# Two transformer blocks on one core: the order of all five engines' work written anew

## The chip, the cores and the metric

The kernel runs on one core of a Trainium2 chip. A core has five engines with instruction streams of their own: TensorE (PE, matmuls; PEld is its weight load), VectorE (DVE), ScalarE (ACT), GpSimd (POOL) and SyncE (SP, which here only issues transfers). They wait for each other by semaphores. Each engine takes its instructions strictly in the order in which they stand in the program, so an instruction that waits holds up all that stand behind it. Transfers between the chip's memory and the core's buffers run on 16 DMA engines and are issued by SyncE and by ScalarE. The metric is the device time of one execution in microseconds (us), the median over several.

## The reference

x has 8 batches of 512 tokens with 256 features. Two layers are added to it, one after the other, and each is a conditioned map and a feed-forward net with ternary weights and 8-bit activations:

```python
x = x + L0_ffn(L0_cond(x, ids0))
x = x + L1_ffn(L1_cond(x, ids1))

L0_cond: h = relu(x @ W1[id] + b1[id]); y = x + h @ W2[id] + b2[id]     # 256 -> 64 -> 256
         layernorm(y) * gamma[id] + beta[id]
L0_ffn:  h = gelu(bitlinear(z, W1, b1)); bitlinear(h, W2, b2)           # 256 -> 1024 -> 256
L1_cond: x @ W[id].T + b[id]                                            # 256 -> 256
L1_ffn:  h = bitlinear(y, w1); h = conv3(h) along the tokens, one filter per channel, + bias
         h = silu(h); bitlinear(h, w2)                                  # 256 -> 1024 -> 256
bitlinear(x, W): W is rounded to -1, 0, 1 times its mean absolute value;
                 x to whole numbers of -128..127 by the largest absolute value of each token
```

The ids pick one of 10 (layer 0) or 8 (layer 1) sets of weights for each batch.

## The kernel before, in words

A batch b is four tiles of 128 tokens; two tiles are a pair p, and the arguments of the functions are (b, p) or (b, tile j). The functions are named after one step each, and each belongs to one engine.

Layer 0, for a batch: SyncE loads the adapter's weights (`load_adapter_weights` L337, `load_second` L345) and gamma and beta (`load_norm` L352), ScalarE issues the loads of x, once transposed (`load_rows` L502) and once as tokens (`load_tokens` L507). PE does `adapter_in` (L1177) and `adapter_out` (L1189), ScalarE the relu between them (`adapter_hidden`). VectorE adds (`add_adapted` L923), centres (`centre` L934) and normalises (`normalise` L943), with the variance from ScalarE (`squares`) and GpSimd (`negative_mean`, `inverse_deviation`). Then the pair is quantised: `absmax_z`, `scale_z`, `inverse_z` on VectorE, `round_z` on ScalarE, `transpose_z` on PE, `untranspose_z` on ScalarE. For each tile PE multiplies (`up1` L1216), ScalarE does `gelu` (L543) into one of two buffers g1, VectorE finds the largest value (`absmax1` L968) and the scale, GpSimd rounds (`round1` L754) into r1, SyncE issues a transposing transfer (`transpose1` L367), PE does `down1` (L1231) and VectorE adds the result to the tokens (`final1` L984). `gelu(b, j)` waits for `round1` of the tile two before, since g1 has two buffers.

Layer 1, for a batch: PE transposes the tokens (`transpose_x` L1262) and multiplies in float32 (`linear` L1279), ScalarE copies in and out (`lead` L574, `evacuate` L580), VectorE finds the scales (`absmax_y` L998), GpSimd rounds (`round_y` L780), PE transposes (`transpose_y`, `spread_scales`), ScalarE copies (`lead_q` L586, `lead_scales`). Then in eight blocks f of 128 channels: `up` on PE (L1326), `dequant` on VectorE (L1014), the three taps of the convolution as `last_tap` on ScalarE (L601), `first_tap` on VectorE (L1021) and `middle_tap` (L798) and, for two blocks at once, `tap_sum` (L808) on GpSimd. For each tile: `transpose_conv` on PE, `silu` on ScalarE, `absmax2` on VectorE, `round2` on ScalarE, `transpose2` by SyncE, `down2` on PE, `final2` on VectorE (L1046) and `store2` by SyncE.

The two layers overlap only at the seam, where the last batches of layer 0 and the first of layer 1 are worked on together. The four weight matrices (1024 KB each) are loaded at the start (`load_weights` L362: n = 0 by ScalarE, 1 to 3 by SyncE), summed by ScalarE (`weight_sum`), totalled by PE (`weight_total`), and made ternary (`weight_scale` and `ternary(0)` on VectorE; `scaled_weights`, `clipped_weights` and `ternary` on ScalarE and GpSimd for the others).

The order of the work is written out by hand for each engine. `run` (L314) goes through four parts:

```python
def run(opening, slot1, closing, slot2):
    opening()
    for s in range(5, B + 1):
        slot1(s)
    closing()
    for s in range(3, B + 4):
        slot2(s)
```

`opening` and `closing` are lists of calls, `slot1` and `slot2` are lists that are repeated for each s, with `on(op, s - 2, j)` calling op for batch s - 2 if there is such a batch. Nothing but these lists sets the order; the waits are inside the functions.

## Time and profile before

| | |
|---|---|
| median of 3 runs | 321.74 us (318.56 to 323.08) |
| the profiled execution | a span of 319.6 us from the first to the last instruction; no time of its own is given beside the span |
| busy: PE, VectorE, ScalarE, GpSimd | 264.5, 276.6, 240.6, 259.2 us |
| moved by transfers | 39.50 MB, 124 GB/s in the mean |

The profile is of one execution. A busy time is the sum of an engine's instructions' durations; an instruction that is held up by another engine once it has started counts as busy. "idle before" in a group of instructions is the time in which the engine had nothing running before them, with what ended most of it. The windows give busy times in stretches of the span, with the granted clock of PE (1.00 is 2.4 GHz) and the DMA engines' share. A transfer's "us to landing" runs from its issue to its arrival.

### The profile page before, as it was taken

To read this page: it belongs to the slowest core of one execution; us is meant where nothing else is said; L and a number is where in the kernel's file an instruction comes from. 1 tells how busy PE (TensorE), PEld (TensorE's weight loads), DVE (VectorE), ACT (ScalarE), POOL (GpSimd) and SP (SyncE) were. 2 spreads that over 40 slices of the span, in tenths; PEclk is the share of its full clock that TensorE was granted. 3 is DMA by queue.
4 is the path that set the end of the run, shared out by engine and by line. 5 is a ranking of instruction groups with operands and counts; after the bars stand their busy time and mean duration, and the time that the engine had idled before them with its cause. 6 is when DMAs were issued, how large, how long until landed. Compare 5 with 4: busy or idle time off the path is not lost. (4 is left out here: it accounts for less than half of the span.)

```text
span 319.6 us, 6460 instructions
## 1 busy us (share of the span) xinstructions
PE 264.5 (83%) x1676; PEld 179.7 (56%) x1700; DVE 276.6 (87%) x606; ACT 240.6 (75%) x366; POOL 259.2 (81%) x402
## 2 busy tenths in 40 slices
PE   6679878869798887999889797989899898967574
PEld 6234334535455454566656665868587686745452
DVE  0778988896899989955899999999999999999671
ACT  4588897966776487567566888889989888978770
POOL 2567899996898988759999999998989799898310
PEclk9977799999999999999999999999999999999997
DMA  7995773579496368454430333445436373444764
GB/s 249 320 363 118 222 197 76 113 159 213 100 215 126 75 87 178 69 100 91 44 66 2 60 74 66 118 98 91 111 93 122 70 98 82 101 98 100 120 145 115
DMA packets 90745, 39.50 MB, mean 124 GB/s; under 512 B 73005, under 2 KB 88141, under 8 KB 90710
## 3 DMA queue, kind: packets, MB, share of 16 engines
q1 hardware_dynamic: 84532, 30.47, 46.8%
q10 hardware_dynamic: 6178, 8.62, 8.6%
q8 instruction: 14, 0.23, 0.3%
q14 instruction: 21, 0.17, 0.2%
HBM read 18.11 MB, written 4.19 MB: 70 GB/s over the span
## 5 line engine op out<-in xcount | busy, mean ns | idle before, releaser
L812 POOL TENSOR_TENSOR raw_all<-raw_all,mid 128x1024 f32<-128x1024 f32 x32 | 63.7, 2000 | 0.7 <-DVE raw_all L1025 0.7
L548 ACT ACTIVATE g<-banks,dqz 128x1024 f32<-128x1024 f32 x32 | 35.5, 1112 | 24.4 <-POOL r L757 21.2
L805 POOL TENSOR_SCALAR mid<-apad,taps,convb 128x512 f32<-128x512 f32 x64 | 48.8, 774 | 0.5 <-DVE apad L1018 0.5
L608 ACT ACTIVATE banks<-apad,taps 128x512 f32<-128x512 f32 x64 | 42.3, 682 | 6.9 <-DVE apad L1018 6.8
L970 DVE TENSOR_REDUCE am<-g 128x1 f32<-128x1024 f32 x32 | 38.6, 1211 | 8.6 <-ACT g L548 8.5
L1025 DVE SCALAR_TENSOR_TENSOR raw_all<-apad,taps,banks 128x512 f32<-128x512 f32 x64 | 45.8, 743 | 0.0
L1018 DVE TENSOR_TENSOR apad<-banks,dqb 128x512 f32<-128x512 f32 x64 | 40.9, 684 | 4.6 <-PE banks L1337 4.5
L757 POOL TENSOR_SCALAR r<-g,qs 128x1024 uint16<-128x1024 f32 x32 | 36.8, 1153 | 6.2 <-DVE qs L982 5.9
L1365 PE MATMUL banks<-tern,q1T 128*128 128x256 bf16 x256 | 33.8, 276 | 9.5 <-DMA q1T<-r 8.0
L1227 PE MATMUL banks<-tern,qT 128*128 128x512 bf16 x117 | 36.6, 388 | 5.5 <-ACT qcT L540 3.3
L627 ACT ACTIVATE r<-g,qs 128x1024 uint16<-128x1024 f32 x32 | 36.6, 1144 | 5.3 <-DVE qs L1044 3.2
L1298 PE MATMUL banks<-wl,x2T 128*128 128x256 f32 x128 | 33.0, 387 | 8.8 <-ACT x2T L577 6.8
L1031 DVE TENSOR_REDUCE am<-g 128x1 f32<-128x1024 f32 x32 | 38.8, 1213 | 1.2 <-ACT g L617 1.2
L1241 PE MATMUL banks<-tern,q1T 128*128 128x256 bf16 x256 | 33.2, 272 | 5.7 <-DVE xs L989 4.1
L1350 PE MATMUL banks<-id,raw_all 128*128 128x128 f32 x256 | 33.5, 274 | 3.6 <-ACT g L617 2.5
L617 ACT ACTIVATE g<-banks 128x1024 f32<-128x1024 f32 x32 | 32.5, 1014 | 4.0 <-PE banks L1350 3.7
L1365 PEld LDWEIGHTS banks<-tern,q1T 128*128 128x128 f16 x256 | 23.8, 98 | 18.5 <-DMA q1T<-r 12.5
L1337 PE MATMUL banks<-yT,tern 128*128 128x512 bf16 x115 | 29.7, 379 | 3.9 <-DVE raw_all L1025 2.4
L1241 PEld LDWEIGHTS banks<-tern,q1T 128*128 128x128 f16 x256 | 24.1, 97 | 15.7 <-issue 6.7
L1350 PEld LDWEIGHTS banks<-id,raw_all 128*128 128x128 f32 x256 | 28.9, 141 | 7.1 <-ACT g L617 3.9
L1298 PEld LDWEIGHTS banks<-wl,x2T 128*128 128x128 f32 x128 | 21.8, 190 | 15.1 <-issue 11.2
L1228 PE MATMUL banks<-bias9b,qcT 128*128 128x512 bf16 x64 | 24.8, 387 | 0.0
(116 smaller groups left out, 561.5 us busy)
## 6 DMA issues: line engine op xcount, KB each, us to landing
out_y<-xs SPq DMA_DIRECT2D x32, 128.0 KB, 2.0
xs<-in_x ACTq DMA_DIRECT2D x7, 512.0 KB, 5.7
x2T<-in_xT ACTq DMA_DIRECT2D x4, 512.0 KB, 5.2
wl<-in_cwl SPq DMA_DIRECT2D x8, 256.0 KB, 2.7
xT<-in_xT ACTq DMA_DIRECT2D x3, 512.0 KB, 4.2
raw_all<-in_w1a ACTq DMA_DIRECT2D x1, 1024.0 KB, 5.0
cw<-in_cw SPq DMA_DIRECT2D x16, 64.0 KB, 5.0
gam<-in_gamma SPq DMA_DIRECT2D x8, 128.0 KB, 3.0
```

The costliest lines, as they stand in the source:

```text
L608: act.activation(bank(BANK_U[g % 3]), apad[:, f, 2:S + 2], ACT.Copy, scale=taps[:, f, 2:3]).then_inc(p_last, 1)
L757: pool.tensor_scalar(r1[j][:, :], g1[j % 2][:, :], qs1[j % 2][:, 0:1], CODE, ALU.mult, ALU.add) \
L805: pool.tensor_scalar(mid[f // 2 % 2][:, f % 2, :], apad[:, f, 1:S + 1], taps[:, f, 1:2], convb[:, f:f + 1], ALU.mult, ALU.add).then_inc(p_ ...
L812: pool.tensor_tensor(c[:, 2 * q:2 * q + 2, :], c[:, 2 * q:2 * q + 2, :], mid[q % 2][:, :, :], ALU.add).then_inc(p_sum, 1)
L970: dve.tensor_reduce(am1[j % 2][:, :], g1[j % 2][:, :], AX_X, ALU.max, apply_absolute_value=True) \
L1018: dve.tensor_tensor(apad[:, f, 1:S + 1], bank(BANK_U[(KH * b + f) % 3]), dqb[b % 2][:, :], ALU.mult) \
L1025: dve.scalar_tensor_tensor(out=conv[b % 2][:, f, :], in0=apad[:, f, 0:S], scalar=taps[:, f, 0:1], in1=bank(BANK_U[(KH * b + f) % 3]), op0= ...
L1031: dve.tensor_reduce(am2[k % 2][:, :], g2[k % 2][:, :], AX_X, ALU.max, apply_absolute_value=True) \
L1241: pe.matmul(o, q1T[j][:, c, :].bitcast(F16), w_dn0[:, c, :], start=(c == 0), stop=False)
L1298: pe.matmul(bank(bank_y(b))[:, a * D:(a + 1) * D], x2T[:, 2 * k + a, j, :], wl1[par][:, j, :], start=(j == 0), stop=False)
L1350: ins = pe.transpose(bank(BANK_C + f // KT)[:, (f % KT) * P:(f % KT + 1) * P], conv[b % 2][:, f, k * P:(k + 1) * P], id32[:, :])
L1365: pe.matmul(o, q2T[k % 2][:, f, :].bitcast(F16), w_dn1[:, f, :], start=(f == 0), stop=False)
```

## The change

No function that computes is changed: the same steps are called, with the same waits (one wait is added: `load2(1)` now also waits for the ids of layer 1, since it may come before `load2(0)`). What changes is the order in which each engine calls them. `opening`, `slot1` and `closing` become one list `first` of each engine, in which every call of layer 0 and of the seam has a place of its own; it reaches on into batch 3 of layer 1. `slot2` has another order and now runs for s of 3 to 8, and the last batches' remaining calls stand in a list `ending`.

```diff
-        def run(opening, slot1, closing, slot2):
-            opening()
-            for s in range(5, B + 1):
-                slot1(s)
-            closing()
-            for s in range(3, B + 4):
+        def run(first, slot2, ending):
+            first()
+            for s in range(3, B + 1):
                 slot2(s)
+            ending()
...
             def load2(b):
                 par = b % 2
-                if b == 0:
+                if b < 2:
                     sp.wait_ge(s_ids, 32)
...
-            def opening():
-                load_adapter_weights(0); load_second(0); load_first_tokens(); load_norm(0)
-                load_adapter_weights(1); load_weights(1); load_second(1); load_weights(2)
-                load_adapter_weights(2); load_norm(1); load_taps(); load_second(2); load_second(3)
...
+            def first():
+                load_adapter_weights(1); load_adapter_weights(0); load_weights(3); load_weights(1); load_norm(1)
+                load_first_tokens(); load_weights(2); load_second(1); load_second(0); load_ids(); load_table()
+                load_taps(); load_norm(0); load_adapter_weights(2); load_second(2); load_adapter_weights(3)
...
+            def ending():
+                transpose2(7, 2); transpose2(7, 3); store2(6, 3); store2(7, 0); store2(7, 2); store2(7, 1)
+                store2(7, 3)
...
-            def opening():
-                weight_sum(0); load_rows(1); bias_leading(); adapter_hidden(0); load_tokens(1); bias_middle()
-                identities(); load_rows(2); squares(0, 0); load_tokens(2); squares(0, 1); adapter_hidden(1)
...
+            def first():
+                load_rows(1); load_tokens(1); weight_sum(0); bias_leading(); identities(); adapter_hidden(0)
+                weight_sum(1); load_rows(2); squares(0, 0); adapter_hidden(1); scaled_weights(1); squares(0, 1)
+                load_tokens(2); weight_sum(2); load_rows(3); bias_middle(); round_z(0, 0); squares(1, 0)
```

Three places show what the lists do. The first is **SyncE's queue at the start of the program** (cw1 and cw2 are the adapter's weights of one batch, in two buffers _0 and _1; raw_all the four weight matrices; xs the tokens). Before:

```order
L342 DMA cw1_0<-in_cw1 128x2x64
...
L349 DMA cw2_0<-in_cw2 64x256
...
L433 DMA xs<-in_x 128x4x256
...
L357 DMA gam0<-in_gamma 128x256
L359 DMA bet0<-in_beta 128x256
...
L342 DMA cw1_1<-in_cw1 128x2x64
...
L363 DMA raw_all<-in_w2a 128x8x256
```

and in the change:

```order
L339 DMA cw1_1<-in_cw1 128x2x64
...
L339 DMA cw1_0<-in_cw1 128x2x64
...
L360 DMA raw_all<-in_w2b 128x8x256
L360 DMA raw_all<-in_w2a 128x8x256
...
L354 DMA gam1<-in_gamma 128x256
L356 DMA bet1<-in_beta 128x256
L420 DMA xs<-in_x 128x4x256
L360 DMA raw_all<-in_w1b 128x2x1024
...
L346 DMA cw2_1<-in_cw2 64x256
...
L346 DMA cw2_0<-in_cw2 64x256
```

Batch 0's second adapter weights (cw2_0), its tokens (xs) and its gamma have moved behind batch 1's and behind the weight matrices.

The second is **VectorE at the start of layer 0** (xx is x plus the adapter's output of pair 0, dqb0 that of pair 1; ws a weight matrix's scale). Before:

```order
L929 SCALAR_TENSOR_TENSOR xx,sums0<-banks,xs 128x256 x2
L939 SCALAR_TENSOR_TENSOR zg<-xx,nmean0,gam0 128x256 x2
L929 SCALAR_TENSOR_TENSOR dqb0,sums1<-banks,xs 128x256 x2
L948 SCALAR_TENSOR_TENSOR z0<-zg,rstd0,bet0 128x256 x2
L954 TENSOR_REDUCE amz0<-z0 128x2
```

and in the change:

```order
L918 SCALAR_TENSOR_TENSOR xx,sums0<-banks,xs 128x256 x2
L918 SCALAR_TENSOR_TENSOR dqb0,sums1<-banks,xs 128x256 x2
L893 TENSOR_SCALAR ws<-banks 128x1
L896 TENSOR_SCALAR thr<-ws 128x1
L897 TENSOR_SCALAR nthr<-ws 128x1
L898 RECIPROCAL iws<-ws 128x1
L928 SCALAR_TENSOR_TENSOR zg<-xx,nmean0,gam0 128x256 x2
L937 SCALAR_TENSOR_TENSOR z0<-zg,rstd0,bet0 128x256 x2
```

The first `centre` (zg) has moved behind both additions and behind the scale of weight matrix 1.

The third is **PE at the seam**, ahead of layer 1's first `up(0, 0)`, the matmuls yT0,tern2 (tern0 with qT1 is `up1`, tern1 with q1T is `down1`, wl1_1 with x2T is `linear(1, 0)`, id32 with xs is `transpose_x(1, 0)`). Before:

```order
L1314 MATMUL banks<-id16,ry 128x128 x8
L1227 MATMUL banks<-tern0,qT1 128x512 x2
...
L1228 MATMUL banks<-bias9b,qcT1 128x512
L1275 MATMUL banks<-id32,xs 128x128 x4
L1337 MATMUL banks<-yT0,tern2 128x512 x6
```

and in the change:

```order
L1281 MATMUL banks<-id16,ry 128x128 x8
L1210 MATMUL banks<-tern0,qT1 128x512 x2
...
L1242 MATMUL banks<-id32,xs 128x128 x4
L1224 MATMUL banks<-tern1,q1T0 128x256 x8
L1225 MATMUL banks<-colsum1,uncode 128x256
...
L1265 MATMUL banks<-wl1_1,x2T 128x256 x2
L1268 MATMUL banks<-table,subjects 128x256
L1304 MATMUL banks<-yT0,tern2 128x512 x6
```

One of the two tiles of `up1` that stood between `transpose_y(0)` (the rows id16,ry) and `up(0, 0)` has moved away, and `down1(6, 0)` and `linear(1, 0)` have moved in.

## Rows read from the trace of the kernel before

**Rows 1.** The page: busy time, share of the span and instructions of each engine.

```profile
PE 264.5 (83%) x1676; PEld 179.7 (56%) x1700; DVE 276.6 (87%) x606; ACT 240.6 (75%) x366; POOL 259.2 (81%) x402
```

**Rows 2.** Windows: stretch, its length, busy time by engine, PE's clock, DMA share, GB/s.

```profile
0.00:20.00 20.00, 12.97 (x46) 7.63 (x46) 9.43 (x21) 10.71 (x20) 7.59 (x18) 0.91 0.95 304
...
20.00:24.00 4.00, 3.08 (x9) 2.35 (x10) 3.31 (x10) 4.00 (x5) 3.77 (x8) 0.73 1.10 342
...
40.00:140.00 100.00, 83.60 (x512) 50.39 (x521) 88.77 (x229) 71.40 (x129) 86.04 (x165) 1.00 0.65 133
140.00:170.00 30.00, 27.26 (x174) 18.55 (x177) 23.43 (x46) 20.56 (x32) 26.84 (x40) 1.00 0.37 63
170.00:300.00 130.00, 112.44 (x811) 86.77 (x821) 127.73 (x240) 111.89 (x147) 120.86 (x147) 1.00 0.43 88
300.00:320.00 20.00, 10.74 (x83) 7.96 (x80) 8.91 (x19) 8.58 (x8) 1.07 (x4) 0.89 0.66 132
```

**Rows 3.** Transfers issued from 0 to 32 us: size, median us to landing.

```profile
raw_all<-in_w2a SPq DMA_DIRECT2D x1, 1024.0 KB, 7.3
...
cw<-in_cw SPq DMA_DIRECT2D x9, 64.0 KB, 6.6
...
xs<-in_x SPq DMA_DIRECT2D x1, 512.0 KB, 6.6
```

**Rows 4.** Timeline of the start: start us, us, engine, line, operation [idle before].

```profile
12.28 1.13 PE L1196 MATMUL banks<-cw,hT 65*128 65x256 f32 x4 [0.78 <-ACT hT L517]
...
13.45 0.42 DVE L929 SCALAR_TENSOR_TENSOR xx<-banks,xs 128x256 f32<-128x256 f32 x1 [1.00 <-PE banks L1196]
...
15.70 3.28 PE L1185 MATMUL banks<-x2T,cw 128*64 128x512 f32 x4
...
26.13 1.63 DVE L921 TENSOR_TENSOR bias9b<-g,bias9b 32x1024 bf16<-32x1024 f32 x1
...
33.92 1.21 DVE L970 TENSOR_REDUCE am<-g 128x1 f32<-128x1024 f32 x1
```

**Rows 5.** Groups of instructions: count | busy us, mean ns | idle before, releasers.

```profile
L812 POOL TENSOR_TENSOR raw_all<-raw_all,mid 128x1024 f32<-128x1024 f32 x32 | 63.7, 2000 | 0.7 <-DVE raw_all L1025 0.7
...
L1025 DVE SCALAR_TENSOR_TENSOR raw_all<-apad,taps,banks 128x512 f32<-128x512 f32 x64 | 45.8, 743 | 0.0
...
L1018 DVE TENSOR_TENSOR apad<-banks,dqb 128x512 f32<-128x512 f32 x64 | 40.9, 684 | 4.6 <-PE banks L1337 4.5
L1031 DVE TENSOR_REDUCE am<-g 128x1 f32<-128x1024 f32 x32 | 38.8, 1213 | 1.2 <-ACT g L617 1.2
L970 DVE TENSOR_REDUCE am<-g 128x1 f32<-128x1024 f32 x32 | 38.6, 1211 | 8.6 <-ACT g L548 8.5
...
L548 ACT ACTIVATE g<-banks,dqz 128x1024 f32<-128x1024 f32 x32 | 35.5, 1112 | 24.4 <-POOL r L757 21.2 <-PE banks L1228 3.1
...
L1298 PE MATMUL banks<-wl,x2T 128*128 128x256 f32 x128 | 33.0, 387 | 8.8 <-ACT x2T L577 6.8 <-issue 2.0
...
L948 DVE SCALAR_TENSOR_TENSOR z<-zg,rstd,bet 128x256 f32<-128x256 f32 x32 | 17.2, 578 | 1.9 <-POOL rstd L723 1.2 <-DVE zg L939 0.7
...
L939 DVE SCALAR_TENSOR_TENSOR zg<-xx,nmean,gam 128x256 f32<-128x256 f32 x16 | 11.1, 733 | 4.1 <-issue 3.7 <-POOL nmean L714 0.4
...
L939 DVE SCALAR_TENSOR_TENSOR zg<-dqb,nmean,gam 128x256 f32<-128x256 f32 x16 | 10.0, 660 | 0.1
```

**Rows 6.** Line L948, `normalise`: duration ns least/median/most.

```profile
L948 DVE SCALAR_TENSOR_TENSOR z<-zg,rstd,bet x32: 459/476/1310, 18.2 to 133.3; 128x256 f32<-128x256 f32 x32
```

**Rows 7.** Timeline of the seam.

```profile
148.26 1.02 ACT L589 ACTIVATE yT<-banks 128x1024 bf16<-128x1024 f16 x1
...
151.72 0.69 DVE L1018 TENSOR_TENSOR apad<-banks,dqb 128x512 f32<-128x512 f32 x1 [3.20 <-PE banks L1337]
```

**Rows 8.** Timeline of the tail: first and last of its nine `final2`.

```profile
295.61 0.48 DVE L1049 SCALAR_TENSOR_TENSOR xs<-banks,dq,xs 128x256 f32<-128x256 f32 x1
...
316.95 0.48 DVE L1049 SCALAR_TENSOR_TENSOR xs<-banks,dq,xs 128x256 f32<-128x256 f32 x1 [2.36 <-PE banks L1366]
```

More of the change, by code:

```diff
@@ L1155, in _ @@
-            run(opening, slot1, closing, slot2)
+                on(scale2, s - 2, 3)
+                on(absmax_y, s + 1)
+                on(first_tap, s, 2)
+                on(inverse2, s - 2, 3)
+                on(scale_y, s + 1)
+                on(dequant, s, 4)
+                on(first_tap, s, 3)
+                on(final2, s - 2, 1)
+                on(inverse_y, s + 1)
+                on(absmax2, s - 1, 0)
+                on(dequant, s, 5)
+                on(scale2, s - 1, 0)
+                on(dequant, s, 6)
@@ L1157, in _, with ending @@
+            def ending():
+                scale2(7, 2); inverse2(7, 2); final2(6, 3); absmax2(7, 3); final2(7, 0); scale2(7, 3); inverse2(7, 3)
+                final2(7, 1); final2(7, 2); final2(7, 3)
+            run(first, slot2, ending)
         @block.tensor
@@ L1413, in _ @@
-            run(opening, slot1, closing, slot2)
+                on(down2, s - 2, 1)
+                on(up, s, 5)
+                on(transpose_conv, s - 1, 1)
+                on(up, s, 6)
+                on(spread_scales, s + 1)
+                on(down2, s - 2, 2)
+                on(transpose_conv, s - 1, 2)
+                on(up, s, 7)
+                on(down2, s - 2, 3)
+                on(transpose_y, s + 1)
+                on(transpose_conv, s - 1, 3)
+                on(transpose_x, s + 2, 0)
@@ L1417, with ending @@
+            def ending():
+                down2(7, 1); down2(7, 2); down2(7, 3)
+            run(first, slot2, ending)
 def kernel(x, itok_B_0_8, itok_B_0_7, L0_cond_W1, L0_cond_b1, L0_cond_W2, L0_cond_b2, L0_cond_gamma,
```

515 lines of the change are left out of this document (230 added, 285 removed).

## The prediction

> **What bounds the kernel now.** I read the busy shares first, then the windows, then who waits for whom inside them, then single instructions where a number was missing. VectorE is the busiest engine, with 276.6 of 319.6 us; GpSimd has 259.2 [rows 1]. No engine's work changes here (the same instructions are issued, in another order), so the time can only move through idle time. Where VectorE is idle is therefore the whole question, and the windows answer it [rows 2]: from 0 to 20 us it works 9.43 us (10.6 idle), from 40 to 140 us, layer 0, 88.77 of 100 (11.2 idle), from 140 to 170, the seam between the layers, 23.43 of 30 (6.6 idle), from 170 to 300, layer 1, 127.73 of 130 (2.3 idle), and in the tail after 300 it works 8.91 us. In layer 1 there is nothing left to win: it is VectorE's own work. GpSimd is the second wall in layer 0 and the seam (86.04 of 100 and 26.84 of 30), so a list that only packs VectorE better soon meets GpSimd: more than about 10 of layer 0's 11.2 us can't be recovered.
>
> The profiled execution spans 319.6 us; the median of the three runs is 321.7, 2.1 above. I make the sum against the span and add 2.1 at the end.
>
> **The front: loads.** What changes most is SyncE's list of transfers. Ahead of `load_second(0)`, without whose weights `adapter_out(0, 0)` can't start, stood the rows of x, one `load_adapter_weights` and nothing large. Now there stand (each size is its shape in four-byte numbers, and the rows give 64, 512 and 1024 KB for three of them [rows 3]) xT 512 KB, two cw of 64, three weight matrices of 1024, gamma and beta of batch 1 with 256, the tokens of batch 0 with 512, and the second weights of batch 1: about 4.7 MB with batch 0's own. ScalarE's queue asks in the same time for w1a, the identity, the biases, xT and tokens of batch 1, another 2.3 MB, since `load_rows(1)` and `load_tokens(1)` have moved ahead of its first sum. That is 7.05 MB. Is the path to memory already full there? Yes: 304 GB/s over the first 20 us at a DMA share of 0.95, then 342 GB/s at 1.10 [rows 2]. 20 us at 304 GB/s is 6.1 MB, and the remaining 0.95 MB at 342 take 2.8: the weights that `adapter_out(0, 0)` needs land at about **22.8 us**. That transfers wait for those ahead shows in a 64 KB load that takes 6.6 us in the median in this stretch, as long as the 512 KB of tokens; a 1 MB weight takes 7.4 [rows 3]. In the trace of before `adapter_out(0, 0)` starts at 12.28 and VectorE's first addition at 13.45 [rows 4], so batch 0 starts some 10.5 us later.
>
> The Trainium skill ("DMA: Bandwidth & Descriptors", Queues, rings and completion order) says that each DMA engine goes round the queues that have work, and takes the descriptors of one ring in order. By that rule too a small load behind three matrices is late, and it speaks against this change; the 6.6 us of the 64 KB load agree.
>
> The lower bound: were the other queue served last, 4.7 MB at 304 GB/s would be there at 15.5, 3.2 us late. The upper: `load_norm(0)` now stands behind the taps as well, and at worst `centre(0, 0)` waits for that too; with a further 3 us, 13.5 late. I take 10.5, since the rates of both queues together fill it exactly.
>
> How much of it reaches the first `absmax1`? From `adapter_out(0, 0)` at 22.8, PE does 1.1, `adapter_in(1)` 3.3 at the clock that this stretch has, and `adapter_out(0, 1)` 1.1 [rows 4]; `weight_scale(1)` has been put ahead of `centre(0, 0)` and needs the total after these: 29.3 with 1 us for both. VectorE's list from there to `absmax1(0, 0)` holds four `centre` and three `normalise` (each 2 x 0.43 from start to start, by the median of 0.476 less the overlap of the next start [rows 4, 6]: 6.0), two `add_adapted` (1.6), three reductions of 512 elements (half the 1.2 of one of 1024 [rows 5]: 1.9), the bias of 1.6 [rows 4] and small ones (0.5): 11.6 us. Waits on ScalarE, whose `weight_sum(2)` and `bias_middle` stand ahead of `round_z(0, 0)`, add at least 0.6. So `absmax1(0, 0)` starts near 41.5, against 33.92 [rows 4]: 7.6 late. One addition (0.8) that was done before it is now done after. **Cost 8.4 us**, bounds 3 and 12. What else was to fill this gap, the weights' sums and scaling on ScalarE, is 2 to 4 us of ScalarE's work, and ScalarE isn't the wall.
>
> **Layer 0.** Two causes of VectorE's idle time are named. `centre` (L939) waited 3.7 us for nothing but a transfer, gamma and beta [rows 5]: `load_norm` stood behind `transpose1(., 2)` in the slot. In the new list `load_norm(5)` stands after `transpose1(2, 0)`, two and more transposes earlier against the `centre` that needs it. I count these 3.7 as gone. `absmax1` (L970) waited 8.5 us for the gelu, and the gelu 21.2 us for GpSimd's rounding [rows 5]: two buffers and a loop through three engines. Between `absmax1(b, 0)` and `absmax1(b, 2)` VectorE has about as much of its own work in the new list as before, and `final1(b, 0)` of the batches 1 to 6 now stands some 3 to 4 us of work later (the durations of what is listed ahead of it, added up in both lists), which gives the transposes and `down1` slack, not the gelu. The bounds are 0 and 8.5; I take 3. `clipped_weights(3)` and `ternary(3)` have moved back by over 20 us of GpSimd's work; they are the same work, and cost nothing as long as layer 1 isn't near: their cover is the 80 us until `dequant(0, 0)`.
>
> **The seam.** `absmax_y(0)` stands after `final1(5, 1)` and no longer after `final1(6, 0)`, ahead of two `absmax1` and three `final1`, 4 us of VectorE's work (2 x 1.2 and 3 x 0.48 [rows 5, 8]). VectorE's longest wait there is 3.20 us, until `up(0, 0)` comes, behind two tiles of `up1` and a transpose on PE; its input, the copy into yT, was done at 149.3 [rows 7]. So the earlier y alone is no gain: PE's place for `up(0, 0)` decides, and there `up1(7, 3)` has gone from ahead of it, but `down1(6, 0)` and `linear(1, 0)` have come. That wait is what is late next. I count **2.5** of the seam's 6.6 us as gone (bounds -2 and 5), since y's earlier start and the missing `up1` together outweigh what has come.
>
> **Layer 1 and the tail.** The new slot has the same distance from `dequant` to `absmax2` to `final2` in batches; PE's `up(s + 1, 4)` is queued behind `transpose_conv(s, 0)`, which needs the last `tap_sum` of batch s; VectorE has four `dequant`, three `first_tap`, two reductions and two `final2` to do meanwhile, 4 x 0.68 + 3 x 0.74 + 2 x 1.2 + 2 x 0.48 = 8.3 us, against two `tap_sum` of 2.0 [rows 5] and a microsecond or two on PE. 0 us, bounds -1 (loss) and 2. In the tail nine `final2` come after the last `first_tap`, from 295.61 to 316.95 [rows 8]. The new list does one `absmax2` of 1.2 earlier and issues the transposes of batch 7 ahead of the stores; the chain transpose, `down2`, `final2` remains. Gain 0.5, bounds 0 and 2.
>
> **The sum.** 319.6 + 8.4 (front) - 3.7 (gamma) - 3.0 (gelu) - 2.5 (seam) - 0.5 (tail) = 318.3 of span, with 2.1 around it **320.4 us**. From the median of before that is -0.4%, no change that can be measured: 2% of 321.7 are 6.4 us, so faster means under 315.3 and slower over 328.2.
>
> **The rivals.**
> 1. *The front isn't paid back* (slower). One mechanism: the operands of batch 0 queue behind three weight matrices, 3 MB. Price at its upper bound 12, or 8.4 with the new lists meeting GpSimd as the next wall, so that the gamma loads alone are won: 321.7 + 12 - 3.7 = 330.0. It decides from the point where `adapter_out(0, 0)` starts after 24 us and VectorE is still idle for over 17 us between 40 and 300. For it: the full DMA queues [rows 2]. Against it: 17.8 us of idle in layer 0 and the seam that were only partly unavoidable.
> 2. *The lists recover nearly everything* (faster). Front at 3, layer 0 down to 4 us of idle, seam and tail with their best: 321.7 + 3 - 7.2 - 5 - 2 = 310.5. For it: one list per engine can put each wait to use, where the slot repeated its own four times; the front has ScalarE's weight work done early. Against it: GpSimd at 86% in the same stretch.
> 3. *PE's place for `up(0, 0)`* turns the seam into a new wait: `up(0, 0)` waits for `linear(1, 0)`, which is 4 x 0.39, and for the gelu of 1.1 that ScalarE does between yT and the copy that `linear` reads [rows 5], with that copy some 3.5 us. The seam then loses 2 instead of winning 2.5. 320.4 + 2.5 + 2 = 324.9.
> 4. *The neighbours decide.* 64 operations of `centre` and `normalise` took 11.1 + 10.0 + 17.2 = 38.3 us [rows 5], where 64 at the median of 0.476 are 30.5 [rows 6]: 7.8 us of VectorE's "busy" time is waiting beside GpSimd's work. The new order sets other neighbours; with half of it gone, 320.4 - 3.9 = 316.5, with half as much again 324.3. The Trainium skill ("SBUF — State Buffer", Who interferes with whom) makes this an exclusive lock, for operations with two SBUF inputs beside a GpSimd operation that reads SBUF, and by that rule reductions are free of it.
>
> **Chances.** Forecast 0.40; rival 1 0.22; rival 2 0.22; rival 3 0.08; rival 4 0.08. Faster by over 2%: rival 2 and a little of rival 4, 0.24. Slower by over 2%: rival 1, 0.22. Within: 0.54. The likeliest case by itself is 316 to 326. To hold 8 in 10 the range must reach into both outer rivals: 311 to 330.
>
> **What would show it.** The first VectorE addition near 24 us, `absmax1(0, 0)` near 41.5; VectorE's idle time 5 in 40 to 140 (shifted by the front's delay) and 4 at the seam; no wait of `centre` for a transfer after batch 0; layer 1 again at 98%. It would be wrong if the first addition came before 17 us, or if VectorE's share in layer 0 stayed under 90% or rose over 95%.

## The result, and the profile after

The change made the kernel slower: 345.55 us (median of 4 runs, 344.75 to 346.29) against 321.59 us for the kernel before, timed on the same chip (4 runs, 318.56 to 323.08). The ratio is 1.0765, interval 1.0689 to 1.0841. I had forecast 320.4 us, within a range of 311 to 330. The profiled execution spans 343.9 us, 24.3 more than the one before. Of the experiments below, e1, e5 and e7 each have one execution that ran at a lower granted clock and about 2% above the fastest of its kernel (342.11, 350.82 and 348.35 us, the last also the profiled one); the medians include it, the ratios don't.

The busy shares come first, since they say whether any engine's work grew:

```profile
PE 271.1 (79%) x1674; PEld 181.8 (53%) x1700; DVE 277.4 (81%) x606; ACT 240.1 (70%) x366; POOL 259.7 (76%) x402
```

VectorE (DVE) works 277.4 us, as against 276.6 [rows 1]: 0.8 of the 24.3 us is longer work, and 23.5 is idle time that it didn't have before. TensorE (PE) is 6.6 us busier with the same matmuls; the windows show where. Their columns are the stretch, its length, each engine's busy time, the granted clock, the DMA share and GB/s:

```profile
0.00:20.00 20.00, 9.16 (x34) 5.99 (x34) 4.56 (x7) 7.47 (x10) 5.20 (x11) 0.71 0.93 297
20.00:24.00 4.00, 0.00 (x0) 0.00 (x0) 0.00 (x0) 1.40 (x2) 0.00 (x0) 0.50 1.06 323
24.00:40.00 16.00, 10.03 (x22) 4.92 (x22) 6.98 (x25) 7.01 (x13) 6.50 (x10) 0.61 0.43 104
40.00:60.00 20.00, 14.64 (x61) 7.15 (x63) 18.04 (x44) 15.45 (x30) 17.15 (x32) 0.76 0.39 113
60.00:140.00 80.00, 66.99 (x402) 40.67 (x408) 74.86 (x191) 58.39 (x115) 67.59 (x136) 1.00 0.62 135
140.00:180.00 40.00, 35.17 (x221) 22.83 (x223) 31.73 (x69) 24.34 (x38) 32.51 (x56) 0.96 0.42 80
180.00:300.00 120.00, 105.37 (x727) 79.04 (x738) 108.04 (x208) 96.11 (x129) 106.35 (x130) 1.00 0.41 77
```

Read against [rows 2]. From 20 to 24 us TensorE, VectorE and GpSimd do nothing while the DMA engines are full (1.06); before, VectorE worked 3.31 of these 4 us. Up to 40 us VectorE now works 11.54 us. Layer 0 proper, 60 to 140, is better than it was: 74.86 of 80 are 94%, where it was 89% [rows 2]. Layer 1 is worse: 108.04 of 120 are 90%, where it was 98%. So there are two separate losses, one at the start and one in layer 1, with a small gain between them.

The start in single instructions, first TensorE and then VectorE (start us, length us, engine, line, operation [idle time before it <- what ended it]). L1168 is `adapter_in`, L1179 `adapter_out`, L918 `add_adapted`, L928 `centre`, L959 `absmax1`:

```profile
13.28 3.67 PE L1168 MATMUL banks<-xT,cw 128*64 128x512 f32 x4 [5.12 <-DMA cw<-in_cw]
26.71 2.04 PE L1179 MATMUL banks<-cw,hT 65*128 65x256 f32 x4 [9.76 <-DMA cw<-in_cb]
28.69 3.68 PE L1168 MATMUL banks<-x2T,cw 128*64 128x512 f32 x4
32.30 1.21 PE L1179 MATMUL banks<-cw,hT 65*128 65x256 f32 x4
```

```profile
28.80 0.42 DVE L918 SCALAR_TENSOR_TENSOR xx<-banks,xs 128x256 f32<-128x256 f32 x1 [16.42 <-PE banks L1179]
...
33.54 0.42 DVE L918 SCALAR_TENSOR_TENSOR dqb<-banks,xs 128x256 f32<-128x256 f32 x1 [3.97 <-PE banks L1179]
...
34.63 1.61 DVE L928 SCALAR_TENSOR_TENSOR zg<-xx,nmean,gam 128x256 f32<-128x256 f32 x2
...
50.92 1.21 DVE L959 TENSOR_REDUCE am<-g 128x1 f32<-128x1024 f32 x1
```

`adapter_out(0, 0)` starts at 26.71 instead of 12.28, the first addition at 28.80 instead of 13.45, and `absmax1(0, 0)` at 50.92 instead of 33.92 [rows 4]: the front costs **17.0 us**. TensorE waits twice for transfers, and its work beside them is dear: after its 9.76 us of idleness the clock stands at 0.50, the lower of its two levels, and the same `adapter_out` takes 2.04 us that took 1.13 before [rows 4].

What released `adapter_out` is the 1 KB row of `load_second(0)`. SyncE's own timeline (SPq: its issuing instructions) tells why it came so late:

```profile
6.19 0.95 SPq L360 DMA_DIRECT2D raw_all<-in_w2b  x1
7.18 1.93 SPq L360 DMA_DIRECT2D raw_all<-in_w2a  x1
9.88 3.31 SPq L354 DMA_DIRECT2D gam<-in_gamma  x1
...
14.41 1.46 SPq L360 DMA_DIRECT2D raw_all<-in_w1b  x1
...
19.28 0.33 SPq L347 DMA_DIRECT2D cw<-in_cb  x1
```

Behind two matrices of 1 MB the issue of a 128 KB load alone holds SyncE for 3.31 us (a load of gamma took 0.36 in the kernel before), and the row's place in the list is later, so it is issued at 19.28 instead of 5.55. Then it is under way for 7.30 us by the chain of waits:

```profile
19.28 7.30 DMA cw<-in_cb
26.58 0.14 issue
26.71 2.04 PE banks L1179 x4
```

Is it the late issue or the bytes ahead that sets the landing? One of the experiments below, e2, has SyncE's loads in the same order and issues the row 2.5 us earlier, and TensorE starts only 0.3 us earlier:

```profile
16.74 0.33 SPq L344 DMA_DIRECT2D cw<-in_cb  x1
```

```profile
26.42 2.05 PE L1143 MATMUL banks<-cw,hT 65*128 65x256 f32 x4 [13.52 <-DMA cw<-in_cb]
```

By 27 us 7.9 MB had been moved in both. So the bytes of both queues set the landing, and the time that SyncE is held in its issues costs little here. The Trainium skill ("DMA: Bandwidth & Descriptors", Queues, rings and completion order) has each ring's descriptors consumed in order; the 7.30 us for 1 KB agree.

Layer 1's loss has one line in the list of waits from 180 to 300 us (engine, line <- releaser: total us, times, longest); the first is VectorE's, the others are those that hang together with it:

```profile
ACT y L562 <- PE banks L1268: 15.6, 12, 1.8
...
PE banks L1304 <- DVE raw_all L1014: 8.1, 12, 1.9
DVE amy L989 <- ACT y L562: 8.1, 6, 1.6
```

From batch 2 on, VectorE waits up to 1.6 us in every batch with `absmax_y` (L989) at the head of its list, for ScalarE's `evacuate` (L562), which waits for TensorE's `linear` (L1268 is its last matmul). One instance:

```profile
249.64 0.75 DVE L1014 SCALAR_TENSOR_TENSOR raw_all<-apad,taps,banks 128x512 f32<-128x512 f32 x1 [0.23 <-ACT banks L587]
250.31 0.69 DVE L1007 TENSOR_TENSOR apad<-banks,dqb 128x512 f32<-128x512 f32 x1
250.91 0.14 DVE L1027 TENSOR_SCALAR s<-am 128x1 f32<-128x1 f32 x1
252.68 1.22 DVE L989 TENSOR_REDUCE amy<-y 128x4 f32<-128x1024 f32 x1 [1.62 <-ACT y L562]
```

Ahead of none of its eight `absmax_y` (L1000) was VectorE idle in the kernel before.

With the starts of `absmax1(0, 0)` and of the eight `absmax_y` as marks the two spans divide so (us; the stretches of each row add up to its span):

| kernel | to absmax1(0,0) | to absmax_y(0) | to absmax_y(3) | to absmax_y(7) | to the end | last batches, each |
|---|---|---|---|---|---|---|
| before | 33.9 | 109.7 | 53.3 | 74.2 | 48.4 | 18.5, 18.3, 18.5 |
| after | 50.9 | 106.9 | 54.7 | 80.3 | 51.1 | 20.3, 20.1, 20.1 |
| difference | +17.0 | -2.8 | +1.4 | +6.0 | +2.7 | +1.7 |

The marks have a fault: the lists moved the marked calls too. So the same stretches by VectorE's work and idle time, from windows cut at the marks (columns as above: the third pair is VectorE's); first before, then after, and of each only the steady part, from `absmax_y(3)` to `absmax_y(7)`, and the tail:

```profile
196.93:271.16 74.23, 67.46 (x491) 53.33 (x497) 73.80 (x141) 65.90 (x89) 69.12 (x86) 1.00 0.49 97
271.16:319.60 48.44, 32.75 (x249) 24.34 (x249) 36.86 (x76) 33.21 (x37) 26.09 (x35) 0.96 0.53 112
```

```profile
212.55:292.82 80.27, 70.91 (x490) 53.04 (x497) 72.02 (x140) 64.83 (x88) 70.39 (x87) 1.00 0.44 88
292.82:343.90 51.08, 35.93 (x258) 25.70 (x259) 40.35 (x81) 36.66 (x41) 29.51 (x39) 0.96 0.54 116
```

| VectorE idle, us | front | to absmax_y(0) | to absmax_y(3) | to absmax_y(7) | to the end |
|---|---|---|---|---|---|
| before | 12.2 | 13.0 | 5.7 | 0.4 | 11.6 |
| after | 29.3 | 10.6 | 7.6 | 8.2 | 10.7 |
| difference | +17.1 | -2.4 | +1.9 | +7.8 | -0.9 |

The tail has lost nothing by waits: it is 2.7 us longer because the new list leaves 3.5 us more of VectorE's work (40.35 against 36.86) behind the last mark. Layer 1's loss is the 7.8 us of the steady part, of which the waits of `absmax_y(4)` to `absmax_y(7)` are 6.2; those of `absmax_y(2)` and `absmax_y(3)`, 0.68 and 1.15, are as much as the seam's 1.9.

The last `absmax_y` themselves started, from batch 4 on, at 215.9, 234.4, 252.7 and 271.2 before, and at 232.4, 252.7, 272.8 and 292.8 after.

### The profile page after: what moved, and what is told of

Read it like the earlier page. It is cut to its first block, busy times and chain, and to the rows that moved or that the text cites. A ratio compares the mean times of both kernels' runs of the same rounds, so it can differ in the third digit from the quotient of the medians.

```text
span 343.9 us, 6459 instructions
## 1 busy us (share of the span) xinstructions
PE 271.1 (79%) x1674; PEld 181.8 (53%) x1700; DVE 277.4 (81%) x606; ACT 240.1 (70%) x366; POOL 259.7 (76%) x402
## 4 chain that ended last, share of the span: by engine, by line
PE 35%; issue 18%; DVE 18%; POOL 10%; SPq 6%; DMA 6%; ACT 4%; DVEq 1%; ACTq 0%; POOLq 0%
PE banks L1265 9%; PE banks L1224 4%; DVE am L1020 4%; DMA q1T<-r 4%; PE banks L1168 3%; PE banks L1304 3%; PE banks L1210 3%; DVE raw_all L1014 3%; PE banks L1332 2%; PE banks L1179 2%; POOL r L748 2%; DMA cw<-in_cb 2%; PE banks L1211 2%; DVE apad L1007 2%; DVE xs L1038 1%
## 5 line engine op out<-in xcount | busy, mean ns | idle before, releaser
L587 ACT ACTIVATE banks<-apad,taps 128x512 f32<-128x512 f32 x64 | 43.4, 690 | 9.4 <-DVE apad L1007 9.4
L1014 DVE SCALAR_TENSOR_TENSOR raw_all<-apad,taps,banks 128x512 f32<-128x512 f32 x64 | 46.6, 740 | 0.9 <-ACT banks L587 0.9
L748 POOL TENSOR_SCALAR r<-g,qs 128x1024 uint16<-128x1024 f32 x32 | 37.9, 1185 | 10.3 <-DVE qs L971 10.1
L1007 DVE TENSOR_TENSOR apad<-banks,dqb 128x512 f32<-128x512 f32 x64 | 42.8, 684 | 2.6 <-PE banks L1304 2.6
L543 ACT ACTIVATE g<-banks,dqz 128x1024 f32<-128x1024 f32 x32 | 35.4, 1110 | 12.7 <-POOL r L748 10.3
L1304 PE MATMUL banks<-yT,tern 128*128 128x512 bf16 x113 | 33.5, 378 | 12.5 <-DVE raw_all L1014 10.8
L959 DVE TENSOR_REDUCE am<-g 128x1 f32<-128x1024 f32 x32 | 38.7, 1210 | 3.3 <-ACT g L543 3.1
L1332 PE MATMUL banks<-tern,q1T 128*128 128x256 bf16 x256 | 33.9, 276 | 8.0 <-DMA q1T<-r 4.2
L1224 PE MATMUL banks<-tern,q1T 128*128 128x256 bf16 x256 | 34.0, 277 | 4.1 <-DMA q1T<-r 2.9
L1317 PE MATMUL banks<-id,raw_all 128*128 128x128 f32 x256 | 34.9, 281 | 1.0 <-ACT g L596 0.7
L1332 PEld LDWEIGHTS banks<-tern,q1T 128*128 128x128 f16 x256 | 24.5, 99 | 16.3 <-DMA q1T<-r 7.0
L1179 PE MATMUL banks<-cw,hT 65*128 65x256 f32 x64 | 19.1, 425 | 16.1 <-DMA cw<-in_cb 9.8
L1224 PEld LDWEIGHTS banks<-tern,q1T 128*128 128x128 f16 x256 | 24.6, 99 | 13.4 <-DMA q1T<-r 4.1
```

The costliest lines, as they stand in the source:

```text
L748: pool.tensor_scalar(r1[j][:, :], g1[j % 2][:, :], qs1[j % 2][:, 0:1], CODE, ALU.mult, ALU.add) \
L1007: dve.tensor_tensor(apad[:, f, 1:S + 1], bank(BANK_U[(KH * b + f) % 3]), dqb[b % 2][:, :], ALU.mult) \
L1014: dve.scalar_tensor_tensor(out=conv[b % 2][:, f, :], in0=apad[:, f, 0:S], scalar=taps[:, f, 0:1], in1=bank(BANK_U[(KH * b + f) % 3]), op0= ...
L1224: pe.matmul(o, q1T[j][:, c, :].bitcast(F16), w_dn0[:, c, :], start=(c == 0), stop=False)
L1304: ins = pe.matmul(bank(BANK_U[g % 3]), w_up1[:, k, f * P:(f + 1) * P], yT[b % 2][:, k, :], start=(k == 0), stop=(k == KD - 1))
L1317: ins = pe.transpose(bank(BANK_C + f // KT)[:, (f % KT) * P:(f % KT + 1) * P], conv[b % 2][:, f, k * P:(k + 1) * P], id32[:, :])
```

## The experiments

The tables below use the same marks, in lengths. In all of them the work is the reference's in full; only the order of calls differs. Two theories stood against each other throughout: that the loss lies in **named places** (SyncE's loads, one place in layer 1's list), and that it lies in **how the five lists fit one another**, so that no single place can be blamed.

### The order of the loads, taken away and put in alone

e1_loads_back is the changed kernel, e2_loads_alone the kernel before; only SyncE's list differs:

```
e1: first():  - load_adapter_weights(1); load_adapter_weights(0); load_weights(3); load_weights(1); ...
              + load_adapter_weights(0); load_second(0); load_first_tokens(); load_norm(0)
              + load_adapter_weights(1); load_weights(1); load_second(1); ...    (old order, 19 calls)
e2: opening(): the reverse, 20 calls
```

> The changed kernel with one engine's list touched: SyncE issues its first 19 loads in the order of the kernel before (batch 0's second adapter matrix, tokens and normalisation vectors ahead of the three weight matrices and of batch 1's loads). Theory A (the order of the loads alone makes the late front): the first addition starts at 13.5 to 15 us instead of 28.8, absmax1(0,0) at 34 to 38 instead of 50.9, and 12 to 17 us come off the total: 329 to 334. Theory B (VectorE's and TensorE's new lists at the start are as much to blame, they put batch 1's work ahead of batch 0's): the first addition is early, but absmax1(0,0) stays behind 42 and the total is above 337. Theory C (what is late in the front is swallowed by waits further on): the front is early and the total within 3 us of 345.6.

> The kernel before with only the changed kernel's order of SyncE's first 20 loads; all other lists as before. Theory A (the loads cost 17 us and nothing hides them): absmax1(0,0) at 48 to 51 instead of 33.9, total 335 to 339. Theory B (the loads are late, but waits of layer 0 in the old lists, some 11 us of VectorE, take up a part): total 326 to 332. Theory C (the front's loss comes from the new lists of the other engines): total within 3 us of 321.6.

e1 took 336.89 us, ratio to the kernel before 1.0512 (1.0377 to 1.0647). e2 took 334.43 us, 1.0427 (1.0312 to 1.0543), 12.7 over its own runs of before.

| kernel | first addition | to absmax1(0,0) | to absmax_y(0) | to absmax_y(3) | to absmax_y(7) | to the end |
|---|---|---|---|---|---|---|
| e1 (after, old loads) | 16.5 | 39.7 | 107.8 | 54.8 | 80.0 | 51.1 |
| e2 (before, new loads) | 28.5 | 48.9 | 108.0 | 52.9 | 74.1 | 49.0 |

The loads alone delay the first addition to 28.5 and `absmax1(0, 0)` by 15.0 us in the old lists; taken out of the new ones they give 11.2 back. e2 hit theory A's start of `absmax1`, and its total lies between A's 335 to 339 and B's 326 to 332: between the marks the late front is paid back by 1.7 us in layer 0 and no more. That was the test of my assumption that later slack would swallow a late start. From the first addition to `absmax1(0, 0)` the old lists take 20.4 us here, as they do in the kernel before (20.5). e1's total, 336.9, missed A's range by 3 us, and so did its start of `absmax1` (39.7 against 34 to 38): 5.8 us of the front stay with the old loads, so they belong to the other engines' lists.

### The remaining 5.8 us of the front

e6_front_moves starts from e1:

```
DVE: - add_adapted(0, 1); weight_scale(1); centre(0, 0); normalise(0, 0); add_adapted(1, 0)
     + add_adapted(0, 1); centre(0, 0); normalise(0, 0); add_adapted(1, 0); weight_scale(1)
PE:  - adapter_out(0, 0); adapter_in(1); adapter_out(0, 1)
     + adapter_out(0, 0); adapter_out(0, 1); adapter_in(1)
ACT: - load_rows(1); load_tokens(1); weight_sum(0); bias_leading(); identities(); adapter_hidden(0)
     + weight_sum(0); load_rows(1); bias_leading(); identities(); adapter_hidden(0); load_tokens(1)
```

> e1_loads_back (the changed kernel with the old order of SyncE's first 19 loads) with four calls more put back: VectorE's weight_scale(1) behind centre(0,0) and not ahead of it, TensorE's adapter_in(1) behind adapter_out(0,1), ScalarE's loads of batch 1's rows and tokens behind its first sum and behind adapter_hidden(0). Theory A (the 5.8 us by which e1's absmax1(0,0) is still behind the kernel before come from these places): centre(0,0) at 14.5 to 16 instead of 22.8, absmax1(0,0) at 34 to 36 instead of 39.7, total 331 to 334. Theory B (they come from the other orders of GpSimd, ScalarE and TensorE behind them): centre(0,0) early, absmax1(0,0) still at 38 to 40, total within 2 us of 336.9.

337.54 us, ratio 1.0545 (1.0455 to 1.0635): no gain. The first addition came at 13.56 and `centre(0, 0)` at 16.57, half a microsecond behind theory A's 14.5 to 16, but `absmax1(0, 0)` at 40.72. The saved time turned into one wait, on VectorE, for what ScalarE had queued behind a transfer:

```profile
22.10 1.63 DVE L911 SCALAR_TENSOR_TENSOR z<-zg,rstd,bet 128x256 f32<-128x256 f32 x2 [4.65 <-POOL rstd L694]
```

```profile
17.93 1.91 ACT L474 ACTIVATE mid<-raw_all 128x2048 bf16<-128x2048 f32 x1 [5.59 <-DMA raw_all<-in_w2a]
```

The second row is `weight_sum(1)`. The new ScalarE list has it, and `scaled_weights(1)`, ahead of batch 0's `squares`; ScalarE stands 5.59 us at it until the matrix lands, and the squares, GpSimd's `rstd` and VectorE's `normalise` are all behind. In e1 it is the same, 5.45 us. Theory B was right on the total, and `absmax1(0, 0)` came even a little behind its 38 to 40.

e9_squares_first is e6 with the first calls of ScalarE and GpSimd as before:

```
ACT:  first 22 calls, POOL: first 16 calls, in the order of the kernel before
      (squares(0, 0); squares(0, 1); adapter_hidden(1) ahead of weight_sum(1))
```

> e6_front_moves with ScalarE's first 22 calls and GpSimd's first 16 in the order of the kernel before. In e6 ScalarE waited 5.6 us for the second matrix (weight_sum(1)) with squares(0,0) behind it, and VectorE's first normalise waited 4.65 us for what comes of those squares. Theory A (that is what held the front): first normalise at 18 to 19 instead of 22.1, absmax1(0,0) at 33.5 to 36 instead of 40.7, total 329 to 332. Theory B (it is TensorE's and VectorE's order behind it): absmax1(0,0) at 38 or later, total above 334.

344.06 us, ratio 1.0769 (1.07 to 1.0838): 6.5 us slower than e6, whose ratio was 1.0545. Theory A missed; theory B's numbers held, and its reason, TensorE's order, is a part of what the trace shows. The first `normalise` did start at 18.15, as A had it, but behind it:

```profile
24.24 0.42 DVE L891 SCALAR_TENSOR_TENSOR xx<-banks,xs 128x256 f32<-128x256 f32 x1 [5.21 <-PE banks L1142]
...
44.57 1.22 DVE L932 TENSOR_REDUCE am<-g 128x1 f32<-128x1024 f32 x1 [7.32 <-ACT g L534]
```

TensorE's list still had `weight_total(1)`, which needs that same `weight_sum(1)`, ahead of `adapter_out(1, 0)`; with the sum later on ScalarE, TensorE stood before it (3.0 us) and VectorE's next addition 5.2. The second row is the larger wait: `absmax1(0, 0)` itself stands 7.32 us for its gelu. In this list `gelu(0, 0)` comes behind `adapter_hidden(2)`, which waited 2.8 us for TensorE, and `ternary(1)`, which waited 1.2 us for GpSimd; in the kernel before `ternary(1)` stood behind it. So `absmax1(0, 0)` fell to 44.6, and a part of that is this mixture, which neither kernel's list has, and not the change itself. A call put back on one engine has to be put back on each engine that has a partner of it.

### How much of the loads is the weights

```
e7_weights_behind (from after), SP:
     - load_adapter_weights(0); load_weights(3); load_weights(1); load_norm(1); load_first_tokens(); load_weights(2)
     + load_adapter_weights(0); load_norm(1); load_first_tokens()
     ...  load_norm(0); + load_weights(3); load_weights(1); load_weights(2)
```

> The changed kernel with only SyncE's three loads of weight matrices (3 MB) moved behind load_norm(0); batch 1's adapter matrices stay ahead of batch 0's. Theory A (it is the megabytes ahead of batch 0's last load that count, at the 300 GB/s the trace shows): 3 MB fewer are 10 us fewer, adapter_out(0,0) at 16 to 18 instead of 26.7, total 334 to 338. Theory B (it is the number of loads issued ahead and their order on the queue): adapter_out(0,0) stays behind 21, total above 340. The ternary work on the second matrix may wait for its load instead: then absmax1(0,0) stays behind 45.

342.81 us, ratio 1.0692 (1.0597 to 1.0788): 2.7 us under the changed kernel by the medians, where A wanted 8 to 12. Of its trace I take only the first 30 us: `adapter_out(0, 0)` started at 16.92, within A's 16 to 18, and the first addition at 19.03 instead of 28.80, the 10 us that 3 MB at 300 GB/s make. But `weight_sum(1)` then waited 10.0 us for its matrix, which ScalarE's list wants ahead of the squares, as the expectation's last sentence had feared. The load order and the front of ScalarE's list belong together: with this list the matrix is urgent whether it is loaded early or late.

### Layer 1: the order taken away and put in alone

Here each kernel is cut at one point. P is the changed kernel's first list on each engine, up to the start of its slot list:

```
e3_layer1_back:   P as changed, then all the rest in the order of the kernel before
e4_layer1_alone:  the calls of P in the order of the kernel before, then the rest as changed
```

> The changed kernel up to the end of its first list on each engine, and from there all that is left in the order of the kernel before (its slot list of layer 1). Theory A (the new slot list of layer 1 costs about 6 us over its steady batches and 2 to 3 at the end): a batch of layer 1 takes 18.4 to 18.8 us instead of 20.2, and the total is 336 to 340. Theory B (layer 1 is slower because of the state it is entered in, or of the clock, not of its order): the total stays within 2 us of 345.6.

> The kernel before in layer 0 and the seam, and the changed kernel's order of layer 1 from the point where its slot list begins. Theory A (the new slot list costs 6 to 9 us): a batch takes about 20 us instead of 18.4 and the total is 327 to 331. Theory B (the slot list as such costs nothing): within 3 us of 321.6.

e3 took 349.70 us, ratio 1.0925 (1.0818 to 1.1033); e4 337.96 us, 1.0546 (1.0439 to 1.0653).

| kernel | to absmax_y(0) from absmax1(0,0) | to absmax_y(3) | batches 3 to 7, each | to the end |
|---|---|---|---|---|
| before | 109.7 | 53.3 | 19.0, 18.5, 18.3, 18.5 | 48.4 |
| after | 106.9 | 54.7 | 19.8, 20.3, 20.1, 20.1 | 51.1 |
| e3 | 109.1 | 56.2 | 28.2, 18.5, 18.3, 18.5 | 47.8 |
| e4 | 110.2 | 57.0 | 21.5, 20.3, 20.1, 20.2 | 52.5 |
| e8 | 105.3 | 69.5 | 18.4, 18.5, 18.2, 18.5 | 47.4 |

The period belongs to the list: 18.4 us with the old order, also behind the changed layer 0 (e3), and 20.2 with the new, also behind the old layer 0 (e4). That refutes theory B of both expectations, for the period. The totals missed theory A. e3's one batch of 28.2 us, and e4's 57.0 and 21.5, come where the two orders meet; I call such a place a joint. My reading, which no run isolates, is that the two orders hold the engines at different distances from one another, and where one follows the other, somebody waits until the distance is made up.

e8_layer1_order_back was to avoid the joint:

```
every engine: the places that layer 1's calls have in the changed list are kept;
              the calls that fill them come in the relative order of the kernel before
```

> The changed kernel with layer 1's calls alone put back: on every engine the places that layer 1's calls have in the changed list are filled with the same calls in the relative order of the kernel before; layer 0 stays as changed. Unlike e3 it has no joint between two orders in mid-layer. Theory A (the new order of layer 1 loses 1.7 us a batch by itself, and e3's long batch of 28 us was its joint): all steady batches at 18.3 to 18.8 us, the steady part 74 to 75.5 us instead of 80.3, total 336 to 340. Theory B (the old order of layer 1 fits only behind the old layer 0): a batch of over 22 us turns up again and the total is 343 or more.

350.49 us, ratio 1.099 (1.0911 to 1.1068). Its row stands in the table above. All four last batches are at 18.2 to 18.5, and the tail is 47.4, as theory A said; the 15 us that the seam got longer are, by my reading, a joint all the same. VectorE waited 4.3 us for a `silu` and 5.0 for a `down1` of layer 0:

```profile
202.35 1.22 DVE L994 TENSOR_REDUCE am<-g 128x1 f32<-128x1024 f32 x1 [4.29 <-ACT g L587]
...
213.31 0.48 DVE L952 SCALAR_TENSOR_TENSOR xs<-banks,dq,xs 128x256 f32<-128x256 f32 x1 [4.99 <-PE banks L1189]
```

Both theories were half right: the batches are theory A's; the total, and a batch of over 22 us (29.8, at the seam), are theory B's. What the windows say of layer 1's steady part (220 to 300 us) is plain: first e8, and then the changed kernel from 240 to 300:

```profile
220.00:300.00 80.00, 73.71 (x534) 58.11 (x533) 79.37 (x151) 71.29 (x97) 73.66 (x92) 1.00 0.49 95
```

```profile
240.00:300.00 60.00, 52.65 (x365) 39.35 (x369) 53.97 (x106) 49.12 (x66) 50.25 (x64) 1.00 0.45 85
```

VectorE is 99% busy with the old order and 90% with the new, at the same granted clock.

### The named place in layer 1

e5_absmax_y_later leaves the changed kernel as it is but for two moves in the slot:

```
DVE:  - on(absmax_y, s + 1)
        on(first_tap, s, 2)
        on(inverse2, s - 2, 3)
      + on(first_tap, s, 3)
      + on(absmax_y, s + 1)
        on(scale_y, s + 1)
        on(dequant, s, 4)
      - on(first_tap, s, 3)
ACT:  + on(last_tap, s, 3)
        on(evacuate, s + 1, 1)
```

> The changed kernel with two moves in its slot list of layer 1: on VectorE absmax_y(s+1) goes behind first_tap(s,2) and first_tap(s,3) instead of ahead of both, and on ScalarE last_tap(s,3) goes ahead of evacuate(s+1,1). Theory A (a batch takes 20.1 us instead of 18.4 because absmax_y stands at the head of VectorE's queue 1.6 us before its input is there, with first_tap(s,2) ready behind it): a batch takes 18.4 to 18.9 us, VectorE's wait on evacuate goes from 1.6 to under 0.4 us, total 334 to 339. Theory B (the loop is TensorE's and ScalarE's: linear, evacuate, lead, with VectorE only waiting for it): VectorE waits elsewhere, a batch stays at 19.5 to 20.2, total 342 to 346.

Its last batches take 19.4, 18.9 and 18.9 us instead of 20.3, 20.1 and 20.1: 1.2 of the 1.7 us are found (the marked call itself moved, but by the same amount in each of these batches). From 180 to 300 us VectorE's wait for `evacuate` fell from 8.1 us in 6 batches to 2.5 in 3 (the changed kernel's row stands further up):

```profile
DVE amy L989 <- ACT y L562: 2.5, 3, 1.7
```

From batch 5 on the wait is gone altogether; two of the three that are left, in batches 2 and 3, stand ahead of the moved calls. What remains of VectorE's waits per batch are 0.2 us of `first_tap` (L1014) for ScalarE and 0.2 of `final2` (L1038) for TensorE, about the 0.5 us by which a batch is still longer than 18.4.

What the total says is less: 345.82 us, ratio 1.0806 (1.0697 to 1.0916), no gain that can be told from the changed kernel's 1.0765. The profiled span is 1.1 us shorter (342.8): layer 1 from `absmax_y(3)` to `absmax_y(7)` 77.2 instead of 80.3, but its front, layer 0 and seam, which the edit doesn't touch but in the last calls, came out 1.1, 0.6 and 0.6 longer in this execution. The expected total of 334 to 339 was wrong by its own arithmetic: the slot list's steady batches are only four to five, and 5 times 1.2 are 6.

### Everything put back at once

```
e10_both_back = e9_squares_first, with e8's order of layer 1
```

> e9_squares_first and e8_layer1_order_back together: loads, first calls and layer 1 as before; what is left of the change is the order of layer 0 behind its front and the way the seam is interleaved. Theory A (the whole loss is front plus layer 1, and layer 0's new lists save the 1 to 3 us that the traces show between absmax1(0,0) and absmax_y(0)): 318 to 323, at or a little under the kernel before. Theory B (layer 0's or the seam's lists cost as well): 325 or more.

347.71 us, ratio 1.0889 (1.083 to 1.0947). Theory A failed. Theory B's number held, but the trace doesn't give it the reason: front 47.5 (e9's wait, 6.28 us here), seam 69.6 (e8's joint), last batches 18.3, 18.4, 18.3, 18.5. Its losses are about those of its two parents together, so it decides nothing about layer 0's lists.

## Why the prediction was wrong

By the terms of its sum:

| term | forecast | measured | 
|---|---|---|
| front, to absmax1(0,0) | +8.4 (3 to 12) | +17.0 |
| layer 0: gamma 3.7, gelu 3.0 | -6.7 | -2.8 |
| seam | -2.5 (-2 to 5 of gain) | +1.4 |
| layer 1 | 0 (-1 to 2 of gain) | +6.0 |
| tail | -0.5 | +2.7 |
| span | 318.3 | 343.9 |

The measured lengths hold the moves of the marks; in VectorE's idle time, the table further up, layer 1 has lost 7.8 us and the tail nothing.

**The front: the mechanism was right, the term was half of what it measured (+8.4 against +17.0), and the error lay in two steps.** The first is the landing. I had 7.05 MB ahead of `adapter_out(0, 0)` and 22.8 us; the trace has it at 26.71. 24 us at the 301 GB/s of the windows are 7.2 MB, and at 222 GB/s up to 26.7 another 0.6: 7.8 MB. The rule was right and my bytes were too few: ScalarE's load of the rows of batch 2, half a megabyte issued at 19.41, wasn't in my sum, and the rate fell from 301 to 222 GB/s at the end. (The 7.4 us that I gave for a 1 MB weight are another matrix's; the row shows 7.3.) That the row was issued late, at 19.28, isn't the reason, as e2 shows, where it was issued at 16.74 and came 0.3 us earlier. The upper bound, 13.5 us late, was short too (14.4). The second step is the way from there to `absmax1(0, 0)`: I had 18.7 us and it took 24.2. The kernel before had itself taken 21.6 us for it (12.28 to 33.92 [rows 4]), so the sum was too short from the start. I priced TensorE's work at the rows of before, `adapter_out` at 1.1 us and `adapter_in` at 3.3; it ran at 2.04 and 3.68, at the lower level of the clock after the idleness that I was forecasting: with the second `adapter_out` 1.4 us more. And I priced VectorE's list at medians, 11.6 us and 0.6 of waits; from 34.63 it took 16.3, since three of the four pairs of `centre` took 1.61, 1.22 and 2.15 us for the 0.86 that I counted, and a `scale_z` that took 0.15 us at its other places in this stretch took 2.08:

```profile
48.93 2.08 DVE L949 TENSOR_SCALAR sz<-amz 128x2 f32<-128x2 f32 x1
```

These are the long "busy" times beside GpSimd's work that my own rival 4 had seen, and that I had left out of this sum. I had also let ScalarE's `weight_sum(1)` ahead of `squares(0, 0)` pass as ScalarE's own 2 to 4 us ("ScalarE isn't the wall"). In the changed kernel that was right, for it was done at 21.4, before anything was there to be squared:

```profile
19.40 1.91 ACT L483 ACTIVATE mid<-raw_all 128x2048 bf16<-128x2048 f32 x1 [1.73 <-DMA raw_all<-in_w2a]
```

With SyncE's loads put back it is 5.45 us (e1) and 5.59 us (e6) of waiting for a transfer, with batch 0 behind. The loads give 15.0 us when they are put into the old lists (e2) and only 11.2 when they are taken out of the new ones (e1): of the 3.8 between them 3.1 are the first addition, which came at 16.52 in e1 and, with ScalarE's two loads of batch 1 moved back as well, at 13.56 in e6.

**Nothing paid it back.** e2 is the clean test: 15.0 us late at `absmax1(0, 0)`, 13.3 longer in span. The old lists' idle time in layer 0 wasn't slack that a late start could use.

**Layer 0: right in direction.** `centre` no longer waits for gamma and beta: the two groups of L928, in the list of groups (count | busy us, mean ns | idle before), read

```profile
L928 DVE SCALAR_TENSOR_TENSOR zg<-xx,nmean,gam 128x256 f32<-128x256 f32 x16 | 10.8, 716 | 0.0
L928 DVE SCALAR_TENSOR_TENSOR zg<-dqb,nmean,gam 128x256 f32<-128x256 f32 x16 | 8.5, 572 | 0.0
...
L959 DVE TENSOR_REDUCE am<-g 128x1 f32<-128x1024 f32 x32 | 38.7, 1210 | 3.3 <-ACT g L543 3.1
```

where it was 3.7 us of "issue" [rows 5], so that term is confirmed. `absmax1`'s wait for the gelu fell from 8.5 to 3.1: 5.4 us gained, more than my 3. What is late next I hadn't named: `final1` (L978) waits 5.2 us for `down1` between 50 and 158 us,

```profile
DVE xs L978 <- PE banks L1225: 5.2, 5, 2.3
```

which the row of 0.6 for the same line in the kernel before wasn't. I had said that `final1`'s later place gives slack to `down1`, the reverse of what came. GpSimd's neighbourhood (rival 4) moved by little over the whole layer: `centre` and `normalise` took 10.8 + 8.5 + 21.4 = 40.7 us instead of 38.3.

**The seam: wrong sign in the row, right at the place.** The wait that I had named, VectorE's for `up(0, 0)`, fell from 3.20 us [rows 7] to 0.91, which is 2.3 of the 2.5 us counted. `dequant(0, 0)` started at 170.38, 12.6 us behind `absmax_y(0)` and no longer 8.1, because five `absmax1` stand between them and no longer two: the mark moved. What took the gain away belongs to layer 1: `absmax_y(2)` and `absmax_y(3)` waited 0.68 and 1.15 us for `evacuate`, the step that failed in layer 1, and one `absmax2` waited 1.2.

**Layer 1: the step that failed.** I wrote that "there is nothing left to win", which was right, and went on to put 0 us on a changed list, with a loss of 1 as the bound, for all of layer 1. I compared distances in batches and checked one pair (`up` behind `transpose_conv`); I didn't ask of each call at the head of VectorE's list when its input is there. With no slack, each microsecond of such a wait is lost in every batch: `absmax_y` at the head 1.6 us early, 1.7 us a batch, 6.0 us in length and 7.8 in idle time over the steady part. e3, e4 and e8 show that this is the list's doing; e5 shows the place, for 1.2 of the 1.7. The tail's +2.7 is no second failure: its idle time fell by 0.9, near the gain of 0.5 that I had counted, and work of the batches before has moved behind the mark.

**Rival 1** had the right sign and the right mechanism, the front not paid back, and its conditions were met (26.71 against 24 us; 27.3 us of idle time between 40 and 300 against 17). It gave 330.0, a front at its bound of 12 with no cost elsewhere; 345.6 is what both failed steps make together. Rival 3 (TensorE's place for `up(0, 0)`) didn't come: that wait became shorter. I had given "slower" 0.22.

What stays open: how much layer 0's changed lists, 2.8 us shorter between the marks, gain by themselves and how much is the effect of starting late. e2 with the old lists is 1.7 shorter there after a late start; e1 with the new lists and most of the late start gone is 1.9 shorter. A kernel with the whole old front on all five engines and e5's moves would tell; it has no measurement, and neither has the price of the three matrices alone in the kernel before. Because of the joints in e3, e8, e9 and e10 no kernel shows both losses gone at once. No version here beats the kernel before.
